# Folding channels and squares in half by accumulating DMAs, in a two-layer block of pixels (24 channels, one core)

## What is computed

```python
x = x + conv_ref(ln_c(x))            # ln_c: mean and variance over the 24 channels
t = tokens(x)
t = t + ffn_ref(ln_t(t), W1, b1, W2, b2)   # 24 -> 96 -> 24, relu
```

## Time and profile before

| | us |
|---|---|
| median of 3 runs | 73.93 (73.73 to 74.59) |
| the profiled execution | 73.69 |
| its span | 71.9 |
| VectorE busy | 60.0 |
| TensorE busy | 51.9 |
| ScalarE busy | 44.6 |
| GpSimd busy (issuing DMAs) | 14.7 |

### The profile page before, as it was taken

The page is one execution under the profiler, slowest core; times in us unless marked ns, Lnnn a source line. Parts: engine busy times, 40 slices in busy tenths (PEclk is TensorE's granted clock), DMA queues, the critical chain, the costliest instruction groups (busy, mean ns, idle before and its releaser), DMA issues.

```text
span 71.9 us, 1322 instructions
## 1 busy us (share of the span) xinstructions
PE 51.9 (72%) x465; PEld 38.4 (53%) x465; DVE 60.0 (83%) x125; ACT 44.6 (62%) x60; POOL 14.7 (20%) x20
## 2 busy tenths in 40 slices
PE   3996999999998999919227993976559367459000
PEld 1335999999995897717005631661518017337000
DVE  2059936999999998999999999999999999996700
ACT  0703242083079996884888699999999995503200
POOL 1000000400030004005131048406054484000000
PEclk9999999999999999999999569999999996555555
DMA  0999993065038001900565319999929999999851
GB/s 12 287 402 406 410 410 142 9 126 92 0 67 152 0 0 29 191 3 0 109 109 137 87 46 285 202 231 270 251 45 273 284 316 207 274 265 250 320 205 55
DMA packets 4619, 12.51 MB, mean 174 GB/s; under 512 B 512, under 2 KB 640, under 8 KB 4608
## 3 DMA queue, kind: packets, MB, share of 16 engines
q0 software_dynamic: 2016, 5.51, 38.1%
q1 hardware_dynamic: 2160, 5.90, 21.7%
q10 hardware_dynamic: 432, 0.97, 3.6%
HBM read 3.72 MB, written 3.15 MB: 96 GB/s over the span
## 4 chain that ended last, share of the span: by engine, by line
DVE 35%; PE 25%; ACT 14%; issue 12%; DMA 7%; DVEq 1%; SPq 1%; ACTq 0%
ACT hidden_rounded L394 11%; DMA pixels<-in_x 7%; PE ps_ffn L578 7%; DVE centred L711 6%; DVE hidden_act L777 6%; PE ps_stats L525 6%; PE ps_ffn L500 4%; DVE result L749 4%; PE ps_hidden L558 4%; DVE hidden_q L786 3%; DVE inv_std L725 2%; DVE square_sums L718 2%; DVE inv_std L754 2%; PE ps_hidden L525 2%; ACT packed_t L385 2%
## 5 line engine op out<-in xcount | busy, mean ns | idle before, releaser
L394 ACT ACTIVATE hidden_rounded<-ps_hidden 128x1024 f16<-128x1024 f32 x24 | 23.3, 1024 | 0.9 <-PE ps_hidden L558 0.8
L558 PE MATMUL ps_hidden<-packed_t,w1q 96*128 96x512 fp8e5 x48 | 14.1, 401 | 5.5 <-ACT hidden_rounded L394 4.5
L578 PE MATMUL ps_ffn<-w2q,hidden_q 128*128 128x96 fp8e5 x192 | 11.7, 228 | 5.2 <-DVE hidden_q L786 4.8
L319 POOL DMA_DIRECT2D result<-pixels x8 | 8.2, 1019 | 34.6 <-DVE result L749 34.4
L578 PEld LDWEIGHTS ps_ffn<-w2q,hidden_q 128*128 128x128 fp8e5 x192 | 10.4, 110 | 8.4 <-DVE hidden_q L786 6.0
L404 ACT ACTIVATE ffn_rounded<-ps_ffn 128x768 f16<-128x768 f32 (+1 forms) x9 | 8.4, 934 | 6.7 <-PE ps_ffn L578 6.7
L777 DVE TENSOR_SCALAR hidden_act<-hidden_rounded,b1q 128x1024 f16<-128x1024 f16 x24 | 11.3, 490 | 0.3 <-issue 0.3
L363 ACT ACTIVATE squares<-centred 128x768 f32<-128x768 f32 (+1 forms) x9 | 6.7, 766 | 7.2 <-DVE centred L711 7.2
L558 PEld LDWEIGHTS ps_hidden<-packed_t,w1q 96*128 96x128 fp8e5 x48 | 3.9, 102 | 10.5 <-ACT hidden_rounded L394 5.5
L786 DVE TENSOR_SCALAR hidden_q<-hidden_act 128x2048 uint16<-128x2048 uint16 (+1 forms) x16 | 8.9, 563 | 0.3
L525 PE MATMUL ps_stats<-squares,fixed 128*128 128x128 f32 x72 | 9.1, 278 | 0.2 <-DVE square_sums L718 0.2
(11 more groups left out here) (46 smaller groups left out, 41.8 us busy)
## 6 DMA issues: line engine op xcount, KB each, us to landing
pixels<-in_x SPq DMA_DIRECT2D x8, 384.0 KB, 6.5
result<-pixels POOLq DMA_DIRECT2D x8, 384.0 KB, 4.6
out<-result SPq DMA_DIRECT2D x7, 384.0 KB, 3.5
result<-ffn_out POOLq DMA_DIRECT2D x6, 384.0 KB, 4.5
fixed<-in_fixed ACTq DMA_DIRECT2D x1, 497.5 KB, 5.5
out<-result ACTq DMA_DIRECT2D x1, 384.0 KB, 3.2
fixed<-in_fixed ACTq DMA_DIRECT2D x1, 64.0 KB, 3.5
```

What stands on the lines that cost most here:

```text
L319: pool.dma_start(result[:, n], pixels[:, n], accum_op=ALU.add).then_inc(s.residual[n], 16)
L394: nc.scalar.activation(hidden_rounded[:, i % HIDDEN_BUFS], ps_hidden[:, i % 2], ACT.Copy).then_inc(s.hidden_rounded, 1)
L558: last = nc.tensor.matmul(ps_hidden[:, i % 2, b * BANK:(b + 1) * BANK], w1q[:, t * P:(t + 1) * P], packed_t[:, n % 2].bitcast(E5M2)[:, b:: ...
L578: last = nc.tensor.matmul(ps_ffn[:, half, at * CQ:(at + 1) * CQ], hidden_q[:, n % 2, t, col * P:(col + 1) * P].bitcast(E5M2)[:, 0::2], w2q ...
```

## The change

1. A new tile `pairs` holds channels 0 to 11 of groups 4 to 7, loaded a second time from x. GpSimd adds channels 12 to 23 to it, from `pixels`, by an accumulating DMA per group (`pair_channels`), at the head of its queue. TensorE's late sum is over 12 matmuls instead of 24 and waits for the four folds.
2. After ScalarE's square of groups 4 to 7, GpSimd adds the upper half of the squares to the lower half (`pair_squares`), and TensorE's sum_squares of these groups has three matmuls instead of six.
3. The peak's PSUM tile is in `ps_turned`; `unevenness` stands before `second_bias(5)` on VectorE.
4. The reciprocals of conv_gain and second_norm are calls of their own, the halves of group 7's second_layer, round_ffn, second_bias and add_ffn too, and the orders of all engines are new.

```diff
+        pairs = sb("pairs", [P, NG - 4, CH, GPIX], F32)
-        ps_peak = ps_stats[0:1, 0:P]
+        ps_peak = ps_turned[0:1, 0:P]
 SP:
             for n in range(NG):
                 sp.dma_start(pixels[:, n], x[n]).then_inc(pixels_in[n], 16)
+                if n >= 4:
+                    sp.dma_start(pairs[:, n - 4], x[n][:, 0:CH]).then_inc(pairs_in[n], 16)
 GpSimd:
+            def pair_channels(n):
+                pool.wait_ge(pixels_in[n], 16)
+                pool.wait_ge(pairs_in[n], 16)
+                pool.dma_start(pairs[:, n - 4], pixels[:, n, CH:C], accum_op=ALU.add).then_inc(pairs_ready[n], 16)
+            def pair_squares(n):
+                pool.wait_ge(squares_ready, steps_before(n) + len(channel_steps(n)))
+                pool.dma_start(squares[:, n, 0:CH * GPIX], squares[:, n, CH * GPIX:], accum_op=ALU.add).then_inc(squares_paired[n], 16)
             def first_groups(s):
+                pair_channels(4)
+                pair_channels(5)
+                pair_channels(6)
+                pair_channels(7)
                 add_pixels(s, 0)
                 add_pixels(s, 1)
+                pair_squares(4)
+                pair_squares(5)
+                pair_squares(6)
+                pair_squares(7)
                 add_pixels(s, 2)
...
                 add_ffn_by_dma(s, 2)
+                add_pixels(s, 6)
                 add_ffn_by_dma(s, 3)
+                add_pixels(s, 7)
                 add_ffn_by_dma(s, 4)
-                add_pixels(s, 6)
                 add_ffn_by_dma(s, 5)
-                add_pixels(s, 7)
 TensorE:
+            def sum_late_channels(part):
+                if part == 0:
+                    for n in range(4, NG):
+                        pe.wait_ge(pairs_ready[n], 16)
+                    pe.wait_ge(sums_taken, 1)
+                for c in range(part * 6, (part + 1) * 6):
+                    last = nc.tensor.matmul(ps_late_channels, ident, pairs[:, :, c, :],
+                                            start=(c == 0), stop=(c == CH - 1))
+                if part == 1:
+                    last.then_inc(sums_ready, 1)
             def find_peak():
                 pe.wait_ge(peak_ready, 1)
-                pe.wait_ge(var_taken, UNITS)
+                pe.wait_ge(flat_pass.turned_copied, NG)
```

More of the change, by code:

```diff
@@ L241, in metaformer_block @@
         pixels_in = [sem(f"pixels_in{n}") for n in range(NG)]
+        pairs_in = {n: sem(f"pairs_in{n}") for n in range(4, NG)}
+        pairs_ready = {n: sem(f"pairs_ready{n}") for n in range(4, NG)}
         ident_in = sem("ident_in")
@@ L254, in metaformer_block @@
         squares_ready = sem("squares_ready")
+        squares_paired = {n: sem(f"squares_paired{n}") for n in range(4, NG)}
         square_sums_ready = sem("square_sums_ready")
@@ L416, in groups @@
                         copy_turned(s, n + 1)
-                    round_ffn(s, n)
+                    for part in range(len(pixel_halves(n))):
+                        round_ffn(s, n, part)
             def first_groups(s):
@@ L562, in first_layer, with second_layer @@
                 last.then_inc(s.first_layer, 1)
-            def second_layer(s, n):
-                pe.wait_ge(s.hidden_q, (n + 1) * 2)
-                if n >= 1:
+            def second_layer(s, n, part=0):
+                lo, hi = pixel_halves(n)[part]
+                if part == 0:
+                    pe.wait_ge(s.hidden_q, (n + 1) * 2)
+                if part == 0 and n >= 1:
                     pe.wait_ge(s.ffn_rounded, n)
-                for i in range(J):
+                for i in range(lo * JP, hi * JP):
                     half, at = divmod(i, JP)
@@ L590, in groups @@
                         turn(s, n + 1)
-                    second_layer(s, n)
+                    for part in range(len(pixel_halves(n))):
+                        second_layer(s, n, part)
                     if n + 1 < NG:
@@ L597, in first_groups @@
                 sum_channels(1)
+                sum_squares(0)
+                sum_squares(1)
+                sum_channels(3)
                 sum_channels(2)
[L599 to L602, removed]
+                sum_late_channels(0)
+                sum_late_channels(1)
                 sum_squares(2)
@@ L611, in first_groups @@
                 first_layer(s, 0, 1)
+                turn(s, 1)
                 sum_squares(4)
                 first_layer(s, 0, 2)
-                turn(s, 1)
                 sum_squares(5)
+                first_layer(s, 1, 0)
                 sum_squares(6)
-                first_layer(s, 1, 0)
                 first_layer(s, 1, 1)
-                sum_squares(7)
                 first_layer(s, 1, 2)
                 turn(s, 2)
+                sum_squares(7)
+                first_layer(s, 2, 0)
+                turn(s, 3)
+                first_layer(s, 2, 1)
+                first_layer(s, 2, 2)
                 pe.wait_ge(second_weights, 1)
@@ L787, in quantise_hidden, with second_bias @@
                                         ALU.mult).then_inc(s.hidden_q, 1)
-            def second_bias(s, n):
+            def second_bias(s, n, part=0):
+                lo, hi = [at * JP // 2 for at in pixel_halves(n)[part]]
                 dve.wait_ge(second_bias_ready, 1)
[L792 to L799, removed]
@@ L801, in add_ffn @@
-            def add_ffn(s, n):
-                dve.wait_ge(s.residual[n], 16)
[L804 to L808, removed]
-                    nc.vector.tensor_tensor(total, total, ffn_out[:, n, :, lo:hi], ALU.add).then_inc(s.result_vector, 1)
+                dve.wait_ge(s.ffn_rounded, n + 1 + part)
+                nc.vector.tensor_tensor(ffn_out[:, n].rearrange("p c (j k) -> p j c k", j=JP)[:, lo:hi],
+                                        ffn_rounded[:, n % 2, lo:hi].rearrange("p j (c q) b -> p j c (q b)", q=Q),
+                                        b2q[:, None, :].broadcast_to([P, hi - lo, 2 * CQ]).rearrange("p j (c k) -> p j c k", k=K),
+                                        ALU.add).then_inc(s.ffn_out, 1)
@@ L811, in unevenness, with add_ffn @@
+            def add_ffn(s, n, part=0):
+                lo, hi = [at * GPIX // 2 for at in pixel_halves(n)[part]]
+                dve.wait_ge(s.residual[n], 16)
+                dve.wait_ge(s.ffn_out, n + 1 + part)
+                total = result[:, n, :, lo:hi]
+                nc.vector.tensor_tensor(total, total, ffn_out[:, n, :, lo:hi], ALU.add).then_inc(s.result_vector, 1)
             def unevenness():
                 xall = xg[:].rearrange("p h s -> p (h s)")
+                dve.wait_ge(inv_std_ready, UNITS)
@@ L970, in groups @@
                         conv(s, n + 1)
-                    second_bias(s, n)
+                    for part in range(len(pixel_halves(n))):
+                        second_bias(s, n, part)
                     if n in ADD_ON_VECTOR:
-                        add_ffn(s, n)
+                        for part in range(len(pixel_halves(n))):
+                            add_ffn(s, n, part)
             def first_groups(s):
```

194 lines of the change are left out of this document (99 added, 95 removed).

## The result

The changed kernel takes **77.83 us** in the median of 4 runs (77.69 to 78.35); the kernel before, beside it on the same chip, 74.06. The ratio is 1.0515, 95% interval 1.0434 to 1.0596: **5% slower**. The profiled execution took 77.95 us, its span is 75.8.

What follows compares the result with a forecast made beforehand. VectorE's in-order queue was taken as the bound. Late sum's end 22.2 + 49.13 + 0.54 - 0.96 = 70.9 against 68.34; with the store +2.7, so 73.69 + 2.7 = 76.4 us, range 73.2 to 78.4.

Steps and rivals of the forecast that it cites:

- last load with the second loads: Landing of the last load in front: 12.2 us, plus 1.9 us for 0.79 MB more in the same queue.
- halved sum at full clock: TensorE's late channel sum over half the matmuls: 5.52 us becomes 2.76.
- end of the late sum: TensorE's late channel sum in front, for which VectorE waits from 18.7 us: ends at 22.2; break-even 19.5.
- Collision: Channel folds issued while loads run displace some of them before the late sum: 1.5 us, bounds 0 to 3.0.
- The fold term: Group 7's channel fold, issue to landing, before the late sum: 3.0 us.
- Clock: TensorE idles before the late sum and its clock falls to half: 0.8 us on the sum, bounds 0 to 2.76.
- From the copy on: From take_sums(3) to VectorE's last add: 49.13 us as before, +0.54 for second_norm(1), -0.96 at the tail.
- The square folds: Folded square sums of groups 4-7: cost nothing, covered by VectorE's own queue with slack 2 us.
- The tail: At the end, moving the peak steps cuts VectorE's idle from 1.36 to 0.4 us: -0.96; crowded stores cost 0.1.
- Rival C: In front, the late sum ends before VectorE arrives at 18.7, and middle idle shrinks: 72.3 us; chance 0.14.
- Rival B: In front, same wait but cheap: no collision, clock stays, fold 2.9; sum ends 19.8, time 74.0 us; chance 0.18.
- D: In front, full collision and a fold of 3.6 us: late sum at 24.3, time 78.5 us; chance 0.15.

Runs made afterwards that it cites:

- loadonly: Changed kernel with the second loads but without the channel folds, so half of the channels are left out of the means: 72.74 us.
- warmgap: Changed kernel with 18 extra pointless matmuls filling TensorE's idle stretch before the late sum: 75.3 us, ratio 1.023 to the kernel before.
- chonly: Changed kernel with the channel folds only, square sums of groups 4-7 over six matmuls: 77.37 us, ratio 1.0528 to the kernel before.
- sqonly: Changed kernel with the square folds only, the channel sum reading the pixels: 74.39 us, ratio 1.0077 to the kernel before.
- best: Changed kernel without either fold, second_inverse(1) and second_norm(1) ahead of take_sums(3) again, second_bias(5) ahead of the peak steps: 73.51 us, ratio 0.9983.
- bias5: Changed kernel with second_bias(5) ahead of the peak steps again, nothing else: 77.98 us, ratio 1.0467 to the kernel before.

## Why the prediction held, step by step

The forecast was 76.4 us in a range of 73.2 to 78.4, slower with a chance of 0.67, by VectorE starving for the channel folds. The place, the sign and the wait are as forecast: the copy (L700 before, L735 now), ended by the late sum. That VectorE's last add came within 0.1 us of the forecast is luck, as the terms show:

| term | forecast | measured | from |
|---|---|---|---|
| last load with the second loads | 14.1 | 14.6 to 14.7 | chain; loadonly |
| collision of folds and loads | 1.5 | 0 | loadonly against the changed kernel |
| landed load to start of the sum | 3.0 | 4.0 | 14.57 to 18.56 |
| halved sum at full clock | 2.8 | 2.9 | warmgap, loadonly |
| the clock | 0.8 | 1.6 | warmgap |
| end of the late sum | 22.2 | 23.1 | chain |
| copy to VectorE's last add | 48.7 | 47.7 | 23.14 to 70.83 |
| VectorE's last add | 70.9 | 70.8 | |
| end of the span behind it | 3.7 | 5.0 | 75.8 - 70.83 |

- **Collision: wrong.** I let the folds displace loads because the row of a transfer showed full engines. The loads kept their 400 GB/s; the folds waited, and the first of them took 4.7 us to land. The fold term is the other side of it: 0.5 us until GpSimd issues, 3.2 to land, 0.25 to start, 1.0 more than I had. With the 0.5 us by which the last load came later, the two errors cancel: the sum began at 18.56 where I had 18.6. That is luck.
- **Clock: right in kind, half in size.** I gave the slow stretch 1.6 us of the sum; from what it cost, it covered about twice 1.6, some 3.2 of the 4.5 us.
- **From the copy on: 1.0 us too long.** I said that nothing takes work off VectorE. From the copy to the last add I had 46.8 us of work from the window before, 0.54 for the norm and 1.3 idle; it was 45.7 of work and 2.0 idle. Over the whole span its busy time fell from 60.0 to 58.3 us, and is 58.1 to 58.4 in every kernel with the new orders and no work added, 60.0 to 60.3 in the two with the old ones. The instructions are the same 125. In the new orders an instruction that doesn't need its predecessor's result often stands between two that do. In the trace before, 37 instructions start within 0.1 us after their predecessor's end and 80 ahead of it; in the changed one 22 and 92. In the trace of the changed kernel such a follower starts 0.08 us before its predecessor's end (59.13 + 0.47 is 59.60, the next starts at 59.52), one that needs it 0.03 to 0.04 us after (65.73 + 0.48 is 66.21, the next starts at 66.25):

```profile
58.04 0.57 DVE L815 TENSOR_SCALAR hidden_act<-hidden_rounded,b1q 128x1024 f16<-128x1024 f16 x1
58.53 0.68 DVE L824 TENSOR_SCALAR hidden_q<-hidden_act 128x2048 uint16<-128x2048 uint16 x1
59.13 0.47 DVE L815 TENSOR_SCALAR hidden_act<-hidden_rounded,b1q 128x1024 f16<-128x1024 f16 x1
59.52 0.41 DVE L824 TENSOR_SCALAR hidden_q<-hidden_act 128x1024 uint16<-128x1024 uint16 x1
59.86 0.47 DVE L815 TENSOR_SCALAR hidden_act<-hidden_rounded,b1q 128x1024 f16<-128x1024 f16 x1
...
65.73 0.48 DVE L815 TENSOR_SCALAR hidden_act<-hidden_rounded,b1q 128x1024 f16<-128x1024 f16 x1
66.25 0.43 DVE L824 TENSOR_SCALAR hidden_q<-hidden_act 128x1024 uint16<-128x1024 uint16 x1
```

Counted over the 125 instructions of both traces, the overlaps of neighbours grew from 6.5 to 7.4 us, and the instructions' own durations fell from 66.5 to 65.7: half of the 1.7 us each. Of the shorter ones, hidden_q in its 128x2048 form went from 703 to 669 ns in the mean, hidden_act from 490 to 476. All profiles agree with the order as the cause of both, but no run changes VectorE's order alone: this is argued, not shown.

- **The square folds: cost nothing beside the channel folds** (chonly against the changed kernel), as forecast; whether they cost up to 0.9 us alone is open (sqonly).
- **The tail: the mechanism right, the give-back mis-sized.** VectorE's tail from the last hidden_q (66.68) to 70.83 is 4.15 us; I had 3.8. But I took 0.1 us for stores 5, 6 and 7 running together, from bounds of 0 to 1.1, because two of them are issued over 1.2 us ahead. The lag is 1.3 us longer than I had (5.0 against 3.7), and 1.0 of it goes with one store or one accumulating transfer less. Group 5's second sum, issued at 57.94 before, is issued at 65.24 now and lands at 68.9, 2.2 us behind the last hidden_q as forecast (2.3); what I had wrong is what the stores then cost. **This term is nearly all by which the total was short:** the profiled execution took 77.95 us, 1.55 over the forecast, of which 1.3 is the lag and 0.35 the time outside the span, 2.15 us here against 1.8, less 0.1 at the last add.

Rival C needed fold 7 to land by 15.9; it landed at 18.3. Rival B had the missing collision right, but needed the clock to stay and the fold to take 2.9 us. Of D only the size came near, and by other terms.

On the Trainium skill's figure (DMA: Bandwidth & Descriptors, Anatomy of one DMA; an estimated 2.45 us for 192 KB), which I had set aside for the rows: the four square folds, issued when the DMA engines had little else, landed in 3.0 to 3.5 us, the channel folds in 3.2 to 4.7. The trace does not agree with it for accumulating transfers; the rows of before were the better guide.

## What to carry to other kernels

Halving an engine's work is worth nothing while another engine is the bound; ask first when the consumer arrives, then what the new producer chain costs from its last input on: here a landed load, an issue, a landing and a sum at the low clock, 8.6 us from the last load to the end of the sum, where it was 6.4 before (12.2 to 18.59). A long wait put ahead of TensorE cost its clock as well as the wait here (1.6 us on one sum), and such a cost can be read by filling the gap with pointless matmuls. Where the last stores meet other transfers, as here, an earlier end of the compute is given back (best: VectorE 1.55 us earlier, the span 0.2) unless those transfers move up as well.

## What the runs showed of the hardware that I had not expected

- Loads in flight kept their rate of 400 GB/s while accumulating DMAs were queued beside them; the folds' traffic appears at 200 GB/s only as the last load's data ends (13.3 us), 2.6 us after the first fold's issue.
- The same 125 VectorE instructions take 1.7 us less busy time in orders that put more independent ones between dependent ones, half of it by overlap and half by shorter instructions; the cause is argued, not isolated.
- A TensorE sum of 24 fp32 records takes 2.92 us at a granted clock of 1.00 and 4.54 when most of it runs at 0.50; in a further profile (bias5, clock 0.50 from 18 to 24 us) it took 5.46.
